# A graph kernel on one Trainium2 core: the second half of the mix layer computed in the edge batches

## The chip, the cores and the metric

The kernel runs on one core of a Trainium2 chip. Its time is in device microseconds (us) of that core, the median of three runs of the same program. Profile and trace come from one further execution, recorded by the hardware profiler. Engines are called by their names: TensorE (PE), VectorE (DVE), ScalarE (ACT), GpSimd (POOL) and SyncE (SP), which here only issues transfers.

## The reference, cut to what matters

`xn` is the layer norm of x, 3125 rows of 256 floats. Three layers are computed from it; the weights are fp32. N = 3125, D = 256, 50,000 edges with three edge types, six node types, eight heads of 32.

```
# edges: every edge takes K and V of its source and Q of its target
K, Q, V = type_proj(xn, node_type, Wk/Wq/Wv)        # a weight matrix for each node type
for t in range(3):
    scores = sum(Wa[t]-turned K[src] * Q[dst], -1) * relation_pri[t] / sqrt(32)
    w      = softmax(scores over all edges of type t)
    msgs  += w * (V[src] @ Wm[t])
gnn = layer_norm(segment_sum(msgs, dst) + xn) * ln_g + ln_b

# mix: linear attention along all rows, then an MLP
q, k, v = split(xn @ Wqkv.T);  q, k = elu(q) + 1, elu(k) + 1
t  = (q @ (k.T v)) / (q . sum(k))
x1 = layer_norm(t + xn) * ln1_g + ln1_b
h  = gelu(x1 @ W1.T + b1)                            # the exact gelu
y  = h @ W2.T + b2
mix = layer_norm(y + x1) * ln2_g + ln2_b

x = x + gnn + mix
x = x + ffn(layer_norm(x))        # up, gelu, down, gated, for the 1561 rows of highest gate score
```

The sums over k and v in the mix attention run over all 3125 rows; the change touches what comes behind x1: h, y and the last layer norm.

## The kernel before

The kernel is written for each engine by hand: every engine has its own program, one instruction behind the other, and semaphores tell an engine when another has done its part. Nothing reorders instructions, so their order in the code of an engine is their order on the chip. The work runs in these stages.

**Front.** x is normalized and node rows are sorted by type.

**Table and mix steps.** A loop of NS + 1 steps runs two things side by side. A tile `t` of 128 sorted nodes gets its K, Q and V rows, which go to tables in DRAM (`kv_scratch`, `q_scratch`); L921 is its K and V product on TensorE, once a step. A tile `m` (NT = 25 of 128 rows) goes through the mix layer, a different part of it in each step: projection and elu, attention, the first layer norm (`shift`, `affine`), `x1T` (the transposed x1, scaled and shifted on ScalarE, L784), `mix_h` (the up product), `gelu` on ScalarE (L794), `mix_y` (the down product), `residual` and `finish` on VectorE (L1300 to L1308: y plus x1 plus bias, statistics, gain), `roots` and `gained` on GpSimd (L667). Exp for the elu and Gelu are in different tables of ScalarE, so that each step has two table loads. The finished row, plus x, goes to `mix_scratch`.

**Edge batches.** 49 batches of eight tiles of 128 edges, as two groups of four tiles. For a group GpSimd issues four gathers of K and V rows from `kv_scratch` (L1425) into a slot of a ring of seven (six in the tensor `big`, one in `wmix`, which held the mix weights). The other engines work on groups of several batches at once, in this order:
- TensorE spreads the target's Q rows (`target_rows`, L1604), sums the messages of a window of targets (`window_sums`, L1621), turns the sums (`turn_sums`, L1630), and makes the types' totals (`totals`, L1639) and maxima (L1648, L1655).
- ScalarE builds the one-hot matrices from distances (L1485 to L1504), copies sums from PSUM (`keep_rows` L1522, `keep_sums` L1528) and takes exponentials (L1513).
- VectorE multiplies K with Q (`products`, L1750), sums per head (L1757), follows the maxima (L1779, L1786, L1793), makes weights (L1800, `mark` L1769), multiplies V by them (`messages`, L1809, two a batch), and searches window bounds (`search`, L1853).
- SP loads the Q rows of windows (L1384) and the keys (L1393).

A slot is free for the next gathers when `window_sums` has read its messages.

**Closing.** The sums of windows are scaled by the softmax factors (VectorE, L2062), turned on TensorE (L2315), copied by ScalarE and stored by SP (L2138) to `agg_scratch`, in 17 units of six groups; `load_part` (L2105) brings the finished mix rows in between, one part of two tiles ahead of each store. GpSimd then gathers the rows (L2203), the second layer norm follows, and the feed-forward layer (L2351 up, L2364 down) ends the kernel.

SP's loop of the closing before the change:

```
for k in range(NU):
    sp.wait_ge(ck_kept, chunks_through(k))      # ScalarE has copied the unit
    ... store of the unit's chunks (L2138) ...
    load_part(k + 2)
    if k == EARLY_AT: ... totals, eight loads of xn rows (L2127) ...
```

Of the kernel before, what the change touches and what calls it, by code (L numbers as in the profile page):

```python
# [10 lines left out]
ALU = mybir.AluOpType  # L11
# [4 lines left out]
P = 128  # L16
# [10 lines left out]
EG = 4  # L27
# [5 lines left out]
RING = 7  # L33
RING_BIG = RING - 1
# [9 lines left out]
SEARCH_AT = 6  # L44
SEARCH_STEPS = 4 + NT + 4
# [30 lines left out]
def build(nc, a, out):  # L76
# [6 lines left out]
    mix_d = scratch("mix_scratch", (NP, D))  # L83
    agg_d = scratch("agg_scratch", (AR, D))
# [5 lines left out]
    with ExitStack() as ctx:  # L90
# [27 lines left out]
        wqT, w1T, w2T = (wmix[:, i * C * D:(i + 1) * C * D].rearrange("p (c o) -> p c o", c=C) for i in range(3))  # L118
        vec_names = ["L0_gnn_ln_g", "L0_gnn_ln_b", "L0_mix_ln2_g", "L0_mix_ln2_b", "L0_mix_b2", "L0_ffn_b2",
# [33 lines left out]
        edge = Arena("edge", 7808)  # L153
# [70 lines left out]
        hT = big.take(2, D)  # L224
        assert big.at <= rel_end
        big.reset(xs_at)
        x2m = big.take(2, D)
        mo = big.take(2, D)
        den = big.take(2, H)
        sts, mvs, rss = big.take(4, 6), big.take(4, 2), big.take(4, 2)  # L230
        nmr = big.take(2)
        x1g = big.take(3, D)
# [16 lines left out]
        kv_slots = [kv[:, s, :, :] for s in range(RING_BIG)] + [wmix[:, :].rearrange("p (k d) -> p k d", k=EG)]  # L249
# [11 lines left out]
        gap = edge.take(4, 64)  # L261
        edge.reset()
# [24 lines left out]
        rows_c = edge.take(NT, D)  # L287
        selT = edge.take(C, ETY, P)
# [10 lines left out]
        junk = edge.take(NHG)  # L299
        edge.reset()  # L300
# [11 lines left out]
        same_t = [vecs[name][0:HW, 0:NHG] for name in ("L0_mix_ln2_g", "L0_mix_ln2_b")]  # L312
        base_f = vecs["L0_mix_b2"][:, 0:NHG + 1]
# [107 lines left out]
        def type_marks(c, dve, in_t, tmp):  # L421
            for t in range(ETY):
# [30 lines left out]
        m_q, m_min, m_exp, m_kf, m_t, m_tx, m_r1, m_rs, m_xh, m_T, m_x1, m_h, m_g, m_y, m_c, m_r2, m_out = (  # L453
            sem(n) for n in ("mix_q", "mix_min", "mix_exp", "mix_kf", "mix_t", "mix_tx", "mix_rstd_1", "mix_shift", "mix_xh",
                             "mix_turned", "mix_x1", "mix_h", "mix_gelu", "mix_y", "mix_stats_2", "mix_rstd_2", "mix_out"))
        m_xin = pair("mix_x_in")
        vmx, pmx, m_xg = sem("mix_step"), sem("mix_pool_step"), sem("mix_x1_gained")
        N_VEC = 5
        mix_vecs = ["L0_mix_b2", "L0_mix_ln2_g", "L0_mix_ln2_b", "L0_gnn_ln_b"]
        mix_vecs += [name for name in vec_names if name in ("L0_mix_ln1_g", "L0_mix_ln1_b")]  # L460
        late_vecs = [name for name in vec_names if name not in mix_vecs]
# [4 lines left out]
        with nc.Block() as block:  # L466
            @block.sync
            def _(sp):
# [88 lines left out]
            def _(pool):  # L557
# [102 lines left out]
                def gained(t):  # L660
                    if t is None:
                        return
                    if t.t == 0:
                        pool.wait_ge(s_pri, 1)
# [1971 lines left out]
```

## Time and profile before

| what | value |
|---|---|
| median of 3 timed runs | 1048.76 us (1048.03 to 1049.56) |
| span of the profiled execution | 1167.3 us |
| TensorE matmul | 967.1 us (83%) |
| VectorE | 803.3 us (69%) |
| GpSimd | 640.5 us (55%) |
| ScalarE | 587.4 us (50%) |
| DMA | 189.89 MB, mean 163 GB/s |

Of the profiled execution there is only the span, 1167.3 us; no time of it by the other clock is shown. It is longer than each of the timed runs, so differences are made against the median and the profile is used for durations and order. The busy shares are averages over stages with different limits.

### The profile page before, as it was taken

To read this page: it belongs to the slowest core of one execution; us is meant where nothing else is said; L and a number is where in the kernel's file an instruction comes from. 1 tells how busy PE (TensorE), PEld (TensorE's weight loads), DVE (VectorE), ACT (ScalarE), POOL (GpSimd) and SP (SyncE) were. 2 spreads that over 40 slices of the span, in tenths; PEclk is the share of its full clock that TensorE was granted. 3 is DMA by queue.
4 is the path that set the end of the run, shared out by engine and by line. 5 is a ranking of instruction groups with operands and counts; after the bars stand their busy time and mean duration, and the time that the engine had idled before them with its cause. 6 is when DMAs were issued, how large, how long until landed. Compare 5 with 4: busy or idle time off the path is not lost.

```text
span 1167.3 us, 18084 instructions
## 1 busy us (share of the span) xinstructions
PE 967.1 (83%) x5053; PEld 677.5 (58%) x5053; DVE 803.3 (69%) x1708; ACT 587.4 (50%) x1534; POOL 640.5 (55%) x818
## 2 busy tenths in 40 slices
PE   5989999997157788777877878778778898999998
PEld 4767777775034444444444444444444687888886
DVE  7755888885256777777767677776767677887541
ACT  2657999983234554555545455554555322322220
POOL 4516788886725666666656666565664025664000
PEclk9999999999565766666667666666776799999999
DMA  9722544444736776766767767677674274210020
GB/s 294 220 71 104 159 145 145 146 146 174 234 114 182 208 212 210 205 204 203 214 202 214 210 198 211 201 211 208 201 211 146 69 226 152 79 46 19 1 86 25
DMA packets 112091, 189.89 MB, mean 163 GB/s; under 512 B 18187, under 2 KB 80734, under 8 KB 111990
## 3 DMA queue, kind: packets, MB, share of 16 engines
q0 software_dynamic: 38992, 129.87, 36.1%
q1 hardware_dynamic: 69718, 55.57, 15.7%
q10 hardware_dynamic: 3280, 3.28, 0.8%
q8 instruction: 43, 0.70, 0.2%
q14 instruction: 58, 0.48, 0.1%
HBM read 154.21 MB, written 34.44 MB: 162 GB/s over the span
## 4 chain that ended last, share of the span: by engine, by line
PE 55%; ACT 12%; issue 11%; another core or an unknown queue 10%; DVE 9%; DMA 1%; SPq 1%; POOL 0%; DVEq 0%; ACTq 0%; POOLq 0%
PE ps L2364 7%; PE ps L1621 7%; PE ps L2351 7%; PE ps L1604 6%; PE ps L921 4%; ACT edge L1500 4%; PE ps L2315 3%; PE ps L932 2%; PE ps L909 2%; PE ps L960 2%; ACT edge L1488 2%; PE ps L985 2%; ACT edge L1485 1%; PE ps L1639 1%
## 5 line engine op out<-in xcount | busy, mean ns | idle before, releaser
L1425 POOL DMA_INDIRECT big<-kv_scratch,src_i x336 | 317.8, 946 | 203.0 <-issue 89.8
L1604 PE MATMUL ps<-edge 64*128 64x256 f32 x784 | 177.6, 595 | 39.0 <-issue 38.8
L1750 DVE TENSOR_TENSOR big<-big,ps 128x1024 f32<-128x1024 f32 x84 | 101.6, 1210 | 121.3 <-PE ps L1604 61.9
L1621 PE MATMUL ps<-big,edge 128*64 128x256 f32 x672 | 149.4, 590 | 19.3 <-issue 10.3
L1604 PEld LDWEIGHTS ps<-edge 64*128 64x128 f32 x784 | 104.7, 289 | 89.5 <-issue 75.1
L1522 ACT ACTIVATE edge<-ps 128x256 f32<-128x256 f32 x98 | 37.6, 383 | 213.3 <-remote 146.0
L1621 PEld LDWEIGHTS ps<-big,edge 128*64 128x64 f32 x672 | 63.2, 199 | 78.6 <-issue 70.0
L1500 ACT ACTIVATE edge<-edge 128x64 f32<-128x64 f32 x392 | 102.9, 334 | 0.0
L1757 DVE TENSOR_REDUCE ps<-big 128x32 f32<-128x1024 f32 x84 | 102.3, 1218 | 0.1
L1809 DVE TENSOR_TENSOR big<-big,ps 128x1024 f32<-128x1024 f32 x84 | 98.9, 1209 | 0.0
L2351 PE MATMUL ps<-big 128*128 128x256 f32 (+2 forms) x416 | 88.7, 368 | 2.8 <-ACT big L2264 2.8
L2364 PE MATMUL ps<-big 128*128 128x256 f32 (+1 forms) x400 | 90.0, 380 | 0.0
L2277 ACT ACTIVATE big<-ps,fb 128x256 f32<-128x256 f32 (+2 forms) x104 | 39.4, 461 | 99.8 <-PE ps L2351 99.8
L1630 PE MATMUL ps<-ident,edge 128*128 128x128 f32 x196 | 53.6, 365 | 41.2 <-ACT edge L1522 32.7
L2351 PEld LDWEIGHTS ps<-big 128*128 128x128 f32 x416 | 74.3, 190 | 11.8 <-ACT big L2264 2.7
L2364 PEld LDWEIGHTS ps<-big 128*128 128x128 f32 (+1 forms) x400 | 73.6, 188 | 10.6 <-issue 0.3
L1425 POOL DMA_INDIRECT wmix<-kv_scratch,src_i x56 | 53.1, 948 | 30.8 <-issue 15.0
L1488 ACT ACTIVATE edge<-edge,ones 128x256 f32<-128x256 f32 x98 | 49.8, 508 | 29.4 <-remote 20.3
L1630 PEld LDWEIGHTS ps<-ident,edge 128*128 128x128 f32 x196 | 23.4, 168 | 68.7 <-ACT edge L1522 51.3
L921 PE MATMUL ps<-big,edge 128*128 x120 | 56.9, 596 | 0.5 <-ACT edge L727 0.3
L1485 ACT ACTIVATE edge<-edge,iota_n 128x256 f32<-128x256 bf16 x98 | 48.7, 497 | 13.9 <-DMA edge<-key_scratch 13.8
L1504 ACT ACTIVATE edge<-edge,ones 128x256 f32<-128x256 f32 x98 | 49.8, 508 | 8.9 <-issue 0.4
(354 smaller groups left out, 1919.0 us busy)
## 6 DMA issues: line engine op xcount, KB each, us to landing
edge<-q_scratch SPq DMA_DIRECT2D x196, 64.0 KB
edge<-key_scratch SPq DMA_DIRECT2D x98, 64.0 KB
big<-kv_scratch,src_i POOLq DMA_INDIRECT x336
agg_scratch<-big SPq DMA_DIRECT2D x16, 252.0 KB
xn_scratch<-big ACTq DMA_DIRECT2D x5, 640.0 KB, 5.4
mix_scratch<-big SPq DMA_DIRECT2D x25, 128.0 KB
big<-xn_scratch SPq DMA_DIRECT2D x25, 128.0 KB, 2.6
edge<-in_x SPq DMA_DIRECT2D x24, 128.0 KB
```

Source lines behind the costliest of these rows:

```text
L921: ins = pe.matmul(ps[1][:, :], xgT[:, t.k, ch * P:(ch + 1) * P], wall[:, ds(ty, 1), ch, 0:2 * D].rearrange("p a o -> p (a o)"), start=(ch ...
L1425: pool.indirect_dma_start(kv_slots[s][:, k, :], None, kv_d[0:N, :], bass.IndirectOffsetOnAxis(ap=src_i[:, e:e + 1], axis=0)).then_inc(got[ ...
L1488: act.activation(ohT[:, g % 2, :], dist, ACT.Relu, bias=ones[:, 0:1], scale=-1.0).then_inc(oh, 1)
L1500: ins = act.activation(gap[:, 2 * k + hg, :], iota_m, ACT.Abs, bias=neg_key[:, e:e + 1])
L1604: ins = pe.matmul(qr_ps[g % 2][:, (2 * hg + k) * D:(2 * hg + k + 1) * D], ohT[64 * hg:64 * hg + 64, g % 2, k * P:(k + 1) * P], qwin[64 * h ...
L1621: ins = pe.matmul(sums_of(g)[64 * hg:64 * hg + 64, :], oneh[:, s, k, hg * 64:hg * 64 + 64], kv_slots[s][:, 2 * hg + k, D:2 * D], start=(k ...
L1630: ins = pe.transpose(sums_of(g)[:, ch * P:(ch + 1) * P], rows_of_sums(g)[:, ch * P:(ch + 1) * P], ident[:, :])
L1750: dve.tensor_tensor(k_rows, k_rows, qr_ps[g % 2].rearrange("p (k d) -> p k d", d=D), ALU.mult).then_inc(pr, 1)
L1757: dve.tensor_reduce(scr[:, g // 2 % 2, (g % 2) * EG * H:(g % 2 + 1) * EG * H].rearrange("p (k h) -> p k h", h=H), kv_slots[g % RING][:, :, ...
L1809: dve.tensor_tensor(v, v, wgt[:, g // 2 % 2, (g % 2) * EG * H:(g % 2 + 1) * EG * H] .rearrange("p (k h d) -> p k h d", h=H, d=1).to_broadc ...
L2351: ins = pe.matmul(hslot[q % 2][:, j * GT * P:j * GT * P + w], fw1[:, ch, f * P:(f + 1) * P], cols[:, ch, at:at + w], start=(ch == 0), stop ...
L2364: ins = pe.matmul(ps[4 + t % 2][0:m, 0:D], fh[:, p % 2, f, at:at + m], fw2[:, f, :], start=(f == 0), stop=(f == FJ - 1))
```

## The change

The mix layer is cut behind x1. In the table steps SP now stores x1T of each tile to DRAM (`mix_x1_scratch`), and the row that goes to `mix_scratch` is only x plus a bias. What follows x1 runs in the edge batches. Tile m belongs to batch F = MIX_FROM[m] = 8 + 3m//2, so 25 of the batches from the eighth on have one. SP loads x1T; at the end of batch F TensorE makes the up product; in batch F + 1 ScalarE makes the gelu and a one-column Exp behind it, TensorE the down product with x1 added by two matmuls with the identity, and VectorE the bias, statistics and gain; SP stores the row to `mix_x2_scratch`. x1T and the row have two places each in `wmix`, so the ring has six slots, all in `big`. In the closing SP loads the rows back two by two behind each store, and GpSimd scales each by its root and adds it to the row of the part (`prepare_row`). VectorE's last combination (`with_rows`) waits for that.

The diff, cut; the new functions are whole but for the fallback of rare inputs, which gets a clearing of semaphores on each engine.

```diff
-RING = 7
-RING_BIG = RING - 1
+RING = 6
+RING_BIG = RING
+MIX_FROM = [8 + 3 * m // 2 for m in range(NT)]
...
@@ SP, table steps
+                    seen(sp, m_x1, t)
+                    sp.dma_start(x1_d[t.t, :, :], x1T[:, t.t % 3, :]).then_inc(m_x1st[t.k], 16)
@@ GpSimd, ScalarE, TensorE, VectorE, table steps: calls taken out
-                    roots(m.at(-5), m_c, m_r2, 1)
-                    gained(m.at(-2))
-                    gelu(m.at(-3))
-                    mix_h(m.at(-3))
-                    mix_y(m.at(-4))
-                    residual(m.at(-5))
-                    finish(m.at(-5))
+                    with_x(m.at(-2))
@@ SP, edge batches
+                def load_x1(m):
+                    at_least(sp, yp, m - 1)
+                    sp.dma_start(x1e[:, m % 2, :], x1_d[m, :, :]).then_inc(x1in[m % 2], 16)
+
+                def store_x2(m):
+                    sp.wait_ge(yg, m + 1)
+                    sp.dma_start(x2_d[m * P:(m + 1) * P, :], x2e[:, m % 2, :]).then_inc(x2st[m % 2], 16)
...
+                    for m in mix_tiles(b, 2):
+                        load_x1(m)
+                    for m in mix_tiles(b, 4):
+                        store_x2(m)
@@ ScalarE, edge batches
+                def mix_gelu(m):
+                    act.wait_ge(hp, m + 1)
+                    at_least(act, yp, m)
+                    for j in range(C):
+                        ins = act.activation(hTe[:, j * P:(j + 1) * P], h_ps_e[:, j * P:(j + 1) * P], ACT.Gelu,
+                                             bias=b1c[:, j:j + 1])
+                    ins.then_inc(hk, 1)
+                    act.activation(back, ones[:, 0:1], ACT.Exp)
...
                     if b >= 0:
                         distances(2 * b + 2)
+                    for m in mix_tiles(b, 1):
+                        mix_gelu(m)
                     keep_rows(2 * b - 3)
@@ TensorE, edge batches
+                def mix_h(m):
+                    pe.wait_ge(x1in[m % 2], 16 * (m // 2 + 1))
+                    at_least(pe, yr, m)
+                    for o in range(C):
+                        for ch in range(C):
+                            ins = pe.matmul(h_ps_e[:, o * P:(o + 1) * P], w1T[:, ch, o * P:(o + 1) * P],
+                                            x1e[:, m % 2, ch * P:(ch + 1) * P], start=(ch == 0), stop=(ch == C - 1))
+                    ins.then_inc(hp, 1)
+
+                def mix_y(m):
+                    pe.wait_ge(hk, m + 1)
+                    for ch in range(C):
+                        pe.matmul(y_ps_e, hTe[:, ch * P:(ch + 1) * P], w2T[:, ch, :], start=(ch == 0), stop=False)
+                    for ch in range(C):
+                        ins = pe.matmul(y_ps_e[:, ch * P:(ch + 1) * P], x1e[:, m % 2, ch * P:(ch + 1) * P], ident[:, :],
+                                        start=False, stop=(ch == C - 1))
+                    ins.then_inc(yp, 1)
...
                     turn_sums(2 * b - 3)
+                    for m in mix_tiles(b, 1):
+                        mix_y(m)
                     totals(b - 1)
                     target_rows(2 * b + 2)
                     window_sums(2 * b - 2)
+                    for m in mix_tiles(b, 0):
+                        mix_h(m)
@@ VectorE, edge batches (mix_row adds the bias, mix_stats, mix_var and mix_gain as their names say)
                     mark(b)
+                    for m in mix_tiles(b, 1):
+                        mix_row(m)
                     messages(2 * b - 2)
+                    for m in mix_tiles(b, 1):
+                        mix_stats(m)
                     messages(2 * b - 1)
+                    for m in mix_tiles(b, 1):
+                        mix_var(m)
+                        mix_gain(m)
@@ SP, closing
+                def load_x2(t):
+                    if t >= NT:
+                        return
+                    at_least(sp, rp, t - 1)
+                    sp.dma_start(x2e[:, t % 2, :], x2_d[t * P:(t + 1) * P, :]).then_inc(x2in[t % 2], 16)
...
+                    load_x2(2 * k + 2)
+                    load_x2(2 * k + 3)
@@ GpSimd, closing
+                def prepare_row(t):
+                    if t >= NT:
+                        return
+                    pool.wait_ge(x2in[t % 2], 16 * (t // 2 + 1))
+                    x2 = x2e[:, t % 2, :]
+                    pool.tensor_scalar(x2, x2, x2r[:, t:t + 1], None, ALU.mult).then_inc(x2g, 1)
+                    pool.wait_ge(mix_in[t // 2 % 3], 16 * (t // 6 + 1))
+                    pool.wait_ge(x2g, t + 1)
+                    pool.tensor_tensor(rows[:, t, :], rows[:, t, :], x2, ALU.add).then_inc(rp, 1)
...
+                for t in range(2 * (HALF_AT + 1)):
+                    prepare_row(t)
@@ VectorE, closing
                 def with_rows(i):
+                    dve.wait_ge(rp, i + 1)
```

ScalarE in an edge batch, before (L1528 copies the turned sums, L1485 and L1488 make distances, L1522 copies window sums, L1513 is the exponential, L1500 and L1504 are one-hots):

```order
L1528 ACTIVATE big<-ps 128x252
L1485 ACTIVATE edge<-edge,iota_n 128x256
L1488 ACTIVATE edge<-edge,ones 128x256
L1522 ACTIVATE edge<-ps 128x256
L1513 ACTIVATE edge<-edge 128x192
L1500 ACTIVATE edge<-edge 128x64 x4
L1504 ACTIVATE edge<-edge,ones 128x256
```

The same place in the first batch with a gelu, with the change; L1500 is now the copy of sums, L1457 and L1460 the distances, L1494 the copy of window sums, L1485 the exponential:

```order
L1500 ACTIVATE big<-ps 128x252
L1457 ACTIVATE edge<-edge,iota_n 128x256
L1460 ACTIVATE edge<-edge,ones 128x256
L1508 ACT_TABLE_LOAD
L1508 ACTIVATE edge<-ps,b1c 128x128 x2
L1511 ACT_TABLE_LOAD
L1511 ACTIVATE edge<-ones 128x1
L1494 ACTIVATE edge<-ps 128x256
L1485 ACTIVATE edge<-edge 128x192
```

Two loads and three activations stand between the distances and the copy of the window sums.

VectorE in an edge batch, before, from the weights of one batch (L1800) to the products of the next (L1750), with one of the search's early steps:

```order
L1800 TENSOR_REDUCE ps<-edge 128x64
L1769 TENSOR_TENSOR edge<-ps,mask 128x192
L1809 TENSOR_TENSOR big<-big,ps 128x4x256 x2
L1835 COPY edge<-ps 124x4
L1836 TENSOR_SCALAR v_L_mix_ln_g<-v_L_mix_b,edge 124x196
```

The same place with the change (L1810 weights, L1779 mark, L1819 messages, L1905 to L1917 the tile's row):

```order
L1810 TENSOR_REDUCE ps<-edge 128x64
L1779 TENSOR_TENSOR edge<-ps,mask 128x192
L1905 TENSOR_TENSOR wmix<-ps,v_L_mix_b 128x256
L1819 TENSOR_TENSOR big<-big,ps 128x4x256
L1909 BN_STATS edge<-wmix 128x6
L1819 TENSOR_TENSOR big<-big,ps 128x4x256
L1913 BN_AGGR v_L_mix_ln_g<-edge 128x2
L1917 SCALAR_TENSOR_TENSOR wmix<-wmix,v_L_mix_ln_g 128x256
L1858 COPY step_f<-edge 128x1
```

The first of the four new operations stands ahead of the messages and needs the down product.

SP at the start of the closing, before: zero rows, then parts of mix rows (L2105) and stores of units (L2138) in turn.

```order
L2129 DMA agg_scratch<-big 128x256
L2130 DMA agg_scratch<-big 69x256
L2105 DMA edge<-mix_scratch 128x2x256 x2
L2138 DMA agg_scratch<-big 126x2x256
L2105 DMA edge<-mix_scratch 128x2x256
```

With the change (L2140 parts, L2155 loads of the mix rows from the edge batches, L2183 stores):

```order
L2170 DMA agg_scratch<-big 128x256
L2171 DMA agg_scratch<-big 69x256
L2140 DMA edge<-mix_scratch 128x2x256 x2
L2155 DMA wmix<-mix_x_scratch 128x256 x2
L2183 DMA agg_scratch<-big 126x2x256
L2140 DMA edge<-mix_scratch 128x2x256
L2155 DMA wmix<-mix_x_scratch 128x256 x2
```

Two loads now stand between each two stores, and each of them waits for a row prepared on GpSimd.

## Rows read from the trace of the kernel before

**Rows 1.** The page, granted TensorE clock in 40 equal slices.

```profile
PEclk9999999999565766666667666666776799999999
```

**Rows 2.** Stretches: from:to, length, busy (count) of PE, PEld, DVE, ACT, POOL; clock; DMA; GB/s.

```profile
97.87:256.40 158.53, 158.06 (x1046) 125.25 (x1045) 125.91 (x359) 147.42 (x284) 125.82 (x173) 1.00 0.41 143
514.70:526.66 11.96, 10.16 (x43) 5.85 (x43) 8.83 (x13) 6.38 (x19) 7.55 (x8) 0.60 0.69 204
342.00:898.30 556.30, 438.82 (x1982) 245.75 (x1984) 402.51 (x585) 294.70 (x874) 347.05 (x372) 0.66 0.69 205
```

**Rows 3.** The page, costliest groups: busy us, mean ns | idle before, releaser.

```profile
L1425 POOL DMA_INDIRECT big<-kv_scratch,src_i x336 | 317.8, 946 | 203.0 <-issue 89.8
...
L1750 DVE TENSOR_TENSOR big<-big,ps 128x1024 f32<-128x1024 f32 x84 | 101.6, 1210 | 121.3 <-PE ps L1604 61.9
```

**Rows 4.** Timeline of two edge batches: start, duration, instruction, idle before.

```profile
504.76 1.08 PE L1621 MATMUL ps<-wmix,edge 128*64 128x256 f32 x8 [0.18 <-issue]
...
510.07 1.97 PE L1621 MATMUL ps<-big,edge 128*64 128x256 f32 x8
...
514.70 0.38 ACT L1522 ACTIVATE edge<-ps 128x256 f32<-128x256 f32 x1 [4.32 <-remote]
514.70 1.22 DVE L1750 TENSOR_TENSOR big<-big,ps 128x1024 f32<-128x1024 f32 x1 [3.54 <-PE ps L1604]
...
516.18 0.94 POOL L1425 DMA_INDIRECT big<-kv_scratch,src_i  x1 [0.30 <-issue]
...
517.38 0.51 ACT L1488 ACTIVATE edge<-edge,ones 128x256 f32<-128x256 f32 x1
...
519.60 0.35 DVE L1793 TENSOR_TENSOR edge<-edge,ps 128x192 f32<-128x192 f32 x1 [0.69 <-issue]
...
521.54 2.34 DVE L1809 TENSOR_TENSOR big<-big,ps 128x1024 f32<-128x1024 f32 x2
...
523.80 0.41 DVE L1853 SCALAR_TENSOR_TENSOR edge<-v_L_mix_b,edge,step_f 128x196 f32<-128x196 f32 x1
```

**Rows 5.** Timeline of ScalarE in a table step: the gelu.

```profile
174.18 1.28 ACT L794 ACT_TABLE_LOAD   x1
175.48 0.63 ACT L794 ACTIVATE big<-ps,b1c 128x128 f32<-128x128 f32 x2
```

**Rows 6.** Timeline of TensorE: L921 in the third and fourth step, and in two later.

```profile
91.49 1.88 PE L921 MATMUL ps<-big,edge 128*128 x4
...
97.87 1.88 PE L921 MATMUL ps<-big,edge 128*128 x4
...
170.03 1.88 PE L921 MATMUL ps<-big,edge 128*128 x4
...
177.27 1.88 PE L921 MATMUL ps<-big,edge 128*128 x4
```

**Rows 7.** Groups on VectorE: the mix row's operations in the table steps.

```profile
L1308 DVE SCALAR_TENSOR_TENSOR big<-big,v_L_mix_ln_g 128x256 f32<-128x256 f32 x25 | 11.5, 460 | 0.0
...
L1300 DVE TENSOR_TENSOR big<-big,v_L_mix_b 128x256 f32<-128x256 f32 x25 | 10.7, 428 | 0.9
...
L1301 DVE BATCH_NORM_STATS2 big<-big 128x6 f32<-128x256 f32 x25 | 10.7, 428 | 0.9
...
L1302 DVE BATCH_NORM_AGGREGATE big<-big 128x2 f32<-128x6 f32 x25 | 4.6, 183 | 0.9
```

**Rows 8.** Timeline of VectorE in the closing: scaling of the units' sums.

```profile
934.42 2.30 DVE L2062 TENSOR_TENSOR big<-big 128x756 f32<-128x756 f32 x2 [0.34 <-PE ps L2315]
...
937.06 2.30 DVE L2062 TENSOR_TENSOR big<-big 128x756 f32<-128x756 f32 x2 [0.34 <-PE ps L2315]
```

**Rows 9.** Groups on GpSimd in the table steps.

```profile
L667 POOL TENSOR_TENSOR big<-big,v_L_mix_ln_g 128x256 f32<-128x256 f32 x25 | 18.0, 719 | 0.1
...
L595 POOL TENSOR_SCALAR edge<-big 128x128 bf16<-128x128 f32 x25 | 16.1, 659 | 6.6 <-DVEq L1092 6.6
```

**Rows 10.** DMA issues of 918 to 975 us: KB each, us to landing.

```profile
big<-xn_scratch SPq DMA_DIRECT2D x8, 128.0 KB, 3.1
```

More of the change, by code:

```diff
@@ L261, in build @@
         gap = edge.take(4, 64)
+        base_f = edge.take(NHG + 1)
+        hTe = edge.take(D)
+        x2s, back = edge.take(6), edge.take(1)
+        assert edge.at <= NT * D + 32
         edge.reset()
@@ L287, in build @@
         rows_c = edge.take(NT, D)
+        edge.take(32)
         selT = edge.take(C, ETY, P)
@@ L299, in build @@
         junk = edge.take(NHG)
+        same_last = edge.take(NHG)
         edge.reset()
@@ L786, in affine @@
                     ins.then_inc(m_x1, 1)
-                def gelu(t):
-                    if t is None:
-                        return
-                    seen(act, m_h, t)
-                    seen(act, m_y, t.at(-2))
-                    for j in range(C):
-                        ins = act.activation(hT[:, t.k, j * P:(j + 1) * P], ps[7][:, j * P:(j + 1) * P], ACT.Gelu,
-                                             bias=b1c[:, j:j + 1])
-                    ins.then_inc(m_g, 1)
                 for s in range(NS + 1):
@@ L1343, in build @@
             s_baseT = sem("bases_turned")
+            x1in, x2st = pair("x1_in"), pair("x2_stored")
+            hp, hk, yp, yr, ya, yv, yg = (sem(n) for n in (
+                "mix_h_ps", "mix_h_gelu", "mix_y_ps", "mix_y_row", "mix_y_stats", "mix_y_var", "mix_y_gained"))
             vd, pd = sem("edge_step"), sem("edge_pool_step")
+            assert [s.num for s in table_sems] == list(range(table_sems[0].num, table_sems[-1].num + 1))
+            for s in table_sems:
+                nc.release_semaphore(s)
+            stage_no[0] += 1
             fb_a, fb_b, fb_c, fb_d, fb_e, fb_f1, fb_g = (sem(n) for n in (
@@ L1369, in build, with mix_tiles @@
             fac_ps = [ps[7][:, 0:ETY * NB], ps[0][:, 0:ETY * NB]]
+            h_ps_e, y_ps_e = ps[0][:, 0:D], ps[0][:, D:2 * D]
+            def mix_tiles(b, lag):
+                return [m for m in range(NT) if MIX_FROM[m] + lag == b]
             def in_range(g):
@@ L2035, in build @@
                 "scaled_first", "scaled_second", "rows_ps", "rows_kept"))
-            ck_st, mix_in = pair("rows_stored"), sem("mix_in")
+            ck_st, mix_in = pair("rows_stored"), [sem(f"x_rows_in{j}") for j in range(3)]
+            x2in, x2g, rp = pair("x2_in"), sem("x2_scaled"), sem("rows_prepared")
+            s_x2r = sem("x2_rstds")
             s_fw, s_head, s_tails = sem("ffn_weights_in"), pair("heads_in"), pair("tails_in")
@@ L2132, in _ @@
                 load_part(1)
+                for i in range(2):
+                    sp.wait_ge(x2st[i], 16 * ((NT + 1 - i) // 2))
+                load_x2(0)
+                load_x2(1)
                 for k in range(NU):
@@ L2215, in _ @@
                 load_tails(0)
+                for t in range(2 * (HALF_AT + 1), 2 * EARLY_AT):
+                    prepare_row(t)
                 pool.wait_ge(sc_first, EARLY_AT)
@@ L2220, in _ @@
                     gather(t)
+                for t in range(2 * EARLY_AT, NT):
+                    prepare_row(t)
                 root(0, v3, mv3, rs3, r3)
```

127 lines of the change are left out of this document (53 added, 74 removed).

## The prediction

> **What bounds the kernel now.** I read the page first, then the stretches of its stages, the groups, and the timeline inside one step of each stage. The page's span is 1167.3 us, and its clock row shows TensorE at full speed for the first ten slices of 29.2 us, at five to seven tenths in the next twenty-one, and full again from about 930 us [rows 1]. The stretches show two regimes [rows 2]: the table and mix steps (97.87 to 256.40) keep TensorE busy 158.06 of 158.53 us and ScalarE 147.42; the edge batches (342 to 898.3) have no engine near full (TensorE 438.8 of 556.3, VectorE 402.5, GpSimd 347.1). The closing behind 919.5 starts with units of row transforms, of which more below.
>
> In the edge batches the reader is to see who waits: VectorE's product of gathered rows (L1750) has 121.3 us idle ahead of it [rows 3], in lumps at the start of each batch. One batch goes from 514.70 to 526.66, 12.0 us. Its start shows VectorE idle 3.54 us and ScalarE 4.32 until the same moment [rows 4]; behind it GpSimd issues eight gathers, 0.946 us each [rows 3] and 0.30 us apart [rows 4], so 8 x 1.25 = 10.0 us. VectorE needs less than that, it is busy 8.83 of the 11.96 us [rows 2].
>
> The profiled execution has only its span to show, and the median of the timed runs is 1048.76 us, 118.5 us less. The idle lumps at L1750 are of just that size [rows 3] (of the batches' groups in slots of `big`; those of the seventh slot come on top); the table steps are filled by TensorE at full clock and have nothing to give. So I take a timed batch to be about 10.0 us, GpSimd's eight gathers, with VectorE 1.2 us below it. Differences worked out below go on the median; on the span they would make 1222 us.
>
> **Table and mix steps.** Removed per tile: eight matmul records of the up product, four of the down product, two gelus, two table loads, the gain and one pair of root operations on GpSimd, five VectorE operations. ScalarE loses 2 x 1.28 us of table loads and 0.63 us of gelu [rows 5]. What a step without the up and down product takes stands in the trace: the third step, whose mix work has not come that far, goes from one L921 to the next in 97.87 - 91.49 = 6.38 us; a full step takes 177.27 - 170.03 = 7.24 us [rows 6]. TensorE is still the bound, so the gain is 0.86 us, not the 3.2 us that ScalarE loses. 22 steps give 19 us, the last ones about 1 more: **-20 us**. Bounds: -12 (if the x1 stores disturb) to -35 (if TensorE's own records alone set the step).
>
> **Edge batches.** 25 of the 49 batches get a tile: two in a row, then one without. VectorE gets four operations: add 0.43, statistics 0.43, aggregate 0.18, gain 0.46 [rows 7], 1.50 us. A batch with a tile is then 8.83 + 1.50 = 10.3 us of VectorE, three batches are 2 x 10.3 + 8.8 = 29.4 against GpSimd's 30.0: own work would be hidden, just. What is not hidden is the wait of VectorE's new first operation for the down product, because VectorE's messages stand behind it. I follow that chain from the end of messages(2b-4), the first of the two in the batch ahead: window sums on TensorE 1.08 at full clock and 0.2 to start; keep_rows, one-hots, keep_sums and distances on ScalarE, from 514.70 to 517.38 + 0.51, 3.2; table load, gelu, table load and a one-column exponential 1.28 + 0.63 + 1.28 + 0.1 = 3.3 [rows 4, 5]; keep_rows 0.38 [rows 4]; on TensorE the turn, the down product, the identity pair and the signal, which I put at 2.1 as an estimate: twice the window sums' 1.08, since the four together stream about twice their columns one after another. Together 10.3 us. In the batch ahead 1.65 us follow messages(2b-4) (one more message, half of 2.34, and the search, 0.41 and its read-out [rows 4]), so the result comes 8.65 us into the batch; VectorE is there after 521.54 - 514.70 less 0.69 idle = 6.15 us [rows 4]. It waits 2.5 us, or 1.3 us in the second batch of a pair, whose forerunner has 1.2 us more behind it. Three batches: 29.4 + 3.8 = 33.2 instead of 30.0, so 3.2 us for two tiles, 12.5 times: 40 us. At the lower clock the same TensorE work takes about twice as long: window sums 1.97 instead of 1.08 [rows 4], in all 2.7 us more per tile, 67 us. I take the full clock nearly alone and put 5 us on: **+45 us**, bounds 0 (the waits fall into idle lumps as those of the profile) and +107.
>
> A table load shows as 1.28 us here, and the next activation starts 0.01 us behind it [rows 5]. The Trainium skill, "ScalarE: Activation LUTs", section "What ACT_TABLE_LOAD costs", counts a drain of about 1.38 us on top, 2.66 us a switch. By that rule each tile would cost 2.8 us more and the edge batches 69 us more; the trace does not agree with it, and the sum goes by the trace.
>
> Six slots instead of seven: a slot's round, from the first gather of a group to the release, takes in this trace seven group times. Behind the issue (5.0 us of four gathers) the rows are wanted two batches ahead of their release; I find no shortage in the timed kernel (20 to 22 us, 5 of issue and about 3 of landing, taken as that of the xn rows, against 30), and put **0** with an upper end of one seventh more time, 100 us if latency alone sets the round.
>
> The x1 loads and x2 stores are 50 x 128 KB on SP's queue, 6.4 MB against some 114 MB that the batches move in 556 us at 205 GB/s [rows 2]: 31 us of transfer at most, hidden while the DMA share is 0.69. SP waits for nothing new that is late.
>
> **Closing.** SP stores a unit of rows each 2.64 us, the spacing of VectorE's scalings of two units (937.06 - 934.42) [rows 8]. In the changed kernel SP must, after each such store, issue two x2 loads, the first only when the row two back is prepared. The round of one of the two buffers is issue 0.4, landing 3.1 as for the xn rows [rows 10], scale, add, then the next issue. The add is 0.72, as the gain on GpSimd was; the scale is 256 wide with a column scalar, which no row shows: at least the 0.66 us of 128 columns, at most twice that, 1.32 us; I take 1.1 [rows 9]. That makes 0.4 + 3.1 + 1.1 + 0.72 + 0.1 = 5.4 us for a unit that took 2.64. Queued behind SP's wait is the next store; ScalarE's copy two units on waits for it, and TensorE for the copy. It holds for units 1 to 11: 11 x 2.75 = 30 us. Before, SP is held up at unit 8 by the early totals and eight xn loads; now it also waits there for GpSimd's five gathers and row 16, and I let the overlap and the new wait cancel: **+30 us**, bounds 0 (short landings, front stores not missed) and +50 (scale and add twice as long beside VectorE's scaling).
>
> **Sum:** -20 + 45 + 0 + 30 = +55; 1048.8 + 55 = 1104 us.
>
> **Rivals.**
> Hidden (faster, 11%): the gelu chain finds its place under GpSimd's 10.0 us a batch, as 29.4 against 30.0 says of the own work, and SP keeps ahead in the closing because x2 rows land in about 1.5 us. Then only the -20 is left: 1029 us, and anything up to 1046. It decides from a wait at the new add of under 0.4 us and a round in the closing under 3 us. Against it: ScalarE's chain is longer than the time that it has.
> Only one of the two costs (27%): the edge batches absorb the tiles, the closing doesn't, or the reverse: 1048.8 - 20 + 30 = 1059, to 1074.
> Low clock or ring (17%): TensorE stays at 1.2 GHz for most of the batches, or six slots become the bound: edge batches +105, 1165 us. For it: the page's clock row [rows 1]; against: the timed batch has not the lumps that the profile's batch has.
> Clock rises (10%): the two window sums near 504.8 and 510.1 ran in 1.08 and 1.97 us at full and half clock [rows 4]. More matmuls in a batch could keep the clock full for more of it, 0.9 us less for each of four such groups; with GpSimd's 10.0 us as floor I count half a us for each of 38 batches back: 1085 us. The Trainium skill, "TensorE: Matmul & The Clock Gate", section "What's actually happening", says that activity releases the throttle and would point to this case.
> The forecast as it stands: 35%.
>
> **Numbers.** 1104 us. The lower neighbours (1059 to 1085) and the upper one up to 1155 belong in the range, which holds about 82%: 1045 to 1158. A measurement of this kernel tells about 0.2%, 2 us, from no change. Slower by more: 0.85; within: 0.03; faster: 0.12.
>
> **What would show it.** After: an L921 spacing near 6.4 us in the table steps; in batches with a tile an idle of 1 to 3 us ahead of the new VectorE add, ended by TensorE; in the closing SP's stores some 5 us apart through unit 11 and ScalarE idle ahead of its copies, ended by those stores. The forecast is wrong if these idles are absent, if gathers become late (VectorE waiting for a landing at L1750), or if the profile's idle lumps exist in timed runs too and swallow the tiles.

## The result, and the profile after

The changed kernel takes **1407.42 us** (median of 4 runs, 1402.84 to 1412.01) against 1048.39 us for the kernel before (1047.73 to 1049.56), a ratio of 1.342 with a 95% interval of 1.338 to 1.345. It is 359 us slower; the forecast was +55, and the range ended at 1158.

The page of the changed kernel: its clock row, as [rows 1], and the groups with the most idle time ahead of them, as [rows 3].

```profile
span 1407.0 us, 18291 instructions
...
PEclk9999999878667676766676676666665897899999
...
L1395 POOL DMA_INDIRECT big<-kv_scratch,src_i x392 | 371.9, 949 | 466.3 <-PE ps L1606 364.4
L1656 PE MATMUL ps<-wmix 128*128 128x128 f32 x200 | 51.9, 441 | 191.3 <-DMA wmix<-mix_x_scratch 191.3
...
L1796 DVE TENSOR_REDUCE mall<-ps 24x1 f32<-24x128 f32 x49 | 13.5, 275 | 235.0 <-PE ps L1633 235.0
```

The gathers (L1395) wait 364 us for window sums, VectorE's maximum (L1796) waits 235 us for TensorE, and TensorE's up product (L1656) waits 191.3 us for x1. I read the first two as consequences and the third as their root, since it is the only one that waits for a transfer and not for another engine; the runs below test that. It is seen in the timeline of one batch F (a selection in order of time, SP's queue among the engines; start, duration, instruction, idle before):

```profile
500.81 0.50 ACT L1457 ACTIVATE edge<-edge,iota_n 128x256 f32<-128x256 bf16 x1
501.33 1.30 SPq L1349 DMA_DIRECT2D edge<-key_scratch  x2
501.76 1.81 PE L1589 MATMUL ps<-edge 64*128 64x256 f32 x8
503.41 4.25 SPq L1340 DMA_DIRECT2D edge<-q_scratch  x4
503.51 1.08 PE L1606 MATMUL ps<-big,edge 128*64 128x256 f32 x8
507.71 0.59 SPq L1354 DMA_DIRECT2D wmix<-mix_x_scratch  x1
511.72 2.08 PE L1656 MATMUL ps<-wmix 128*128 128x128 f32 x8 [7.13 <-DMA wmix<-mix_x_scratch]
...
516.67 0.28 DVE L1796 TENSOR_REDUCE mall<-ps 24x1 f32<-24x128 f32 x1 [8.39 <-PE ps L1633]
```

The x1 load of a tile stands in turn F + 2 of SP's loop. That turn starts with the keys, whose slot is free when ScalarE has read the old ones for the second distances of batch F (501.3). Behind them stand four Q window issues (to 507.7), and only then the x1 load. It lands at 511.7; TensorE wanted it at 504.6 and has the next batch's target rows queued behind the up product.

The stages by the marks of the timelines: the table steps end (first product of the edge batches) at 278.8 us instead of 301.9, and L910, the old L921, comes each 6.37 us instead of 7.24 [rows 6]:

```profile
168.00 1.88 PE L910 MATMUL ps<-big,edge 128*128 x4
174.37 1.88 PE L910 MATMUL ps<-big,edge 128*128 x4
```

In the edge batches those ahead of the first tile take some 10 us (9.9 to 10.4 from the fourth to the eighth), later ones with a tile some 26 and 22.5 us in turn, and those without 9 us. Stretches of the changed kernel, edge batches and closing (columns as in [rows 2]):

```profile
278.80:1108.20 829.40, 502.20 (x2455) 332.56 (x2456) 458.65 (x706) 387.97 (x1031) 365.19 (x389) 0.69 0.52 153
1108.20:1214.40 106.20, 66.48 (x469) 59.38 (x469) 59.65 (x80) 20.40 (x61) 71.81 (x69) 0.83 0.47 142
```

One thing is needed to read the runs below. They fell on several chips, and the kernel before took 1171.67 us on one, 1175.46 on another and 1049.23 on a third. The first two are called "long" chips below, and the third, like the one of the main result, a "short" chip. The profile before, 1167.3 us long, is by its batches from a long chip: a batch takes 12.1 us in it, and 10 us in the profiles from the short chip. Times are compared with the kernel before on the same chip, and stages of profiles only within one kind.

### The profile page after: what moved, and what is told of

It reads as the page before. It is cut to its first block, busy times and chain, and to the rows that moved or that the text cites. A ratio compares the mean times of both kernels' runs of the same rounds, so it can differ in the third digit from the quotient of the medians.

```text
span 1407.0 us, 18291 instructions
## 1 busy us (share of the span) xinstructions
PE 979.9 (70%) x5153; PEld 720.0 (51%) x5153; DVE 786.3 (56%) x1657; ACT 605.3 (43%) x1565; POOL 654.6 (47%) x795
## 4 chain that ended last, share of the span: by engine, by line
PE 41%; ACT 12%; DMA 10%; SPq 10%; issue 10%; POOL 9%; DVE 7%; DVEq 0%; ACTq 0%; POOLq 0%
DMA wmix<-mix_x_scratch 9%; PE ps L2420 6%; PE ps L2433 6%; POOL big L1395 5%; PE ps L1589 5%; SPq L1340 4%; PE ps L1656 4%; PE ps L910 3%; SPq L1339 3%; SPq L1349 2%; ACT L1511 2%; ACT L1508 2%; POOL wmix L2230 2%; PE ps L949 2%; PE ps L1606 2%
## 5 line engine op out<-in xcount | busy, mean ns | idle before, releaser
L1395 POOL DMA_INDIRECT big<-kv_scratch,src_i x392 | 371.9, 949 | 466.3 <-PE ps L1606 364.4
L1656 PE MATMUL ps<-wmix 128*128 128x128 f32 x200 | 51.9, 441 | 191.3 <-DMA wmix<-mix_x_scratch 191.3
L1589 PE MATMUL ps<-edge 64*128 64x256 f32 x784 | 170.7, 575 | 16.4 <-DMA edge<-q_scratch 12.7
L1606 PE MATMUL ps<-big,edge 128*64 128x256 f32 x784 | 133.7, 472 | 26.1 <-ACT big L1500 17.0
L1656 PEld LDWEIGHTS ps<-wmix 128*128 128x128 f32 x200 | 44.5, 328 | 205.5 <-DMA wmix<-mix_x_scratch 205.5
L1500 ACT ACTIVATE big<-ps 128x252 f32<-128x252 f32 x98 | 35.9, 368 | 261.3 <-PE ps L1615 261.3
L1796 DVE TENSOR_REDUCE mall<-ps 24x1 f32<-24x128 f32 x49 | 13.5, 275 | 235.0 <-PE ps L1633 235.0
L1760 DVE TENSOR_TENSOR big<-big,ps 128x1024 f32<-128x1024 f32 x98 | 118.6, 1211 | 16.0 <-DMA big<-kv_scratch,src_i 12.1
L1767 DVE TENSOR_REDUCE ps<-big 128x32 f32<-128x1024 f32 x98 | 119.4, 1218 | 0.1
L1819 DVE TENSOR_TENSOR big<-big,ps 128x1024 f32<-128x1024 f32 x98 | 116.5, 1208 | 0.0
L1494 ACT ACTIVATE edge<-ps 128x256 f32<-128x256 f32 x98 | 37.1, 379 | 139.6 <-PE ps L1606 139.6
L2384 PE MATMUL ps<-bd_m,big 128*126 128x128 f32 (+1 forms) x396 | 53.0, 301 | 22.1 <-ACT big L2319 20.6
```

What stands on the lines that cost most here:

```text
L1395: pool.indirect_dma_start(kv_slots[s][:, k, :], None, kv_d[0:N, :], bass.IndirectOffsetOnAxis(ap=src_i[:, e:e + 1], axis=0)).then_inc(got[ ...
L1589: ins = pe.matmul(qr_ps[g % 2][:, (2 * hg + k) * D:(2 * hg + k + 1) * D], ohT[64 * hg:64 * hg + 64, g % 2, k * P:(k + 1) * P], qwin[64 * h ...
L1606: ins = pe.matmul(sums_of(g)[64 * hg:64 * hg + 64, :], oneh[:, s, k, hg * 64:hg * 64 + 64], kv_slots[s][:, 2 * hg + k, D:2 * D], start=(k ...
L1656: ins = pe.matmul(h_ps_e[:, o * P:(o + 1) * P], w1T[:, ch, o * P:(o + 1) * P], x1e[:, m % 2, ch * P:(ch + 1) * P], start=(ch == 0), stop=( ...
L1760: dve.tensor_tensor(k_rows, k_rows, qr_ps[g % 2].rearrange("p (k d) -> p k d", d=D), ALU.mult).then_inc(pr, 1)
L1767: dve.tensor_reduce(scr[:, g // 2 % 2, (g % 2) * EG * H:(g % 2 + 1) * EG * H].rearrange("p (k h) -> p k h", h=H), kv_slots[g % RING][:, :, ...
```

## The experiments

**1. On a long chip (before: 1171.67 us).** The x1 load one turn earlier:

```diff
-                    for m in mix_tiles(b, 2):
+                    for m in mix_tiles(b, 1):
                         load_x1(m)
```

> The changed kernel with the load of x1 issued one turn of SP's loop earlier, and nothing else changed. Theory A, the load comes too late: the profile of the changed kernel shows TensorE idle 191.3 us ahead of the up product, 25 times 7.65 us, until that load has landed. Without it the idle is gone, and with it what the other engines and the ring lose by it: at least 191 us less, 1216 us, and down to about 1100 us if the rest of a long batch (26.0 and 22.5 us against 9.1 us for one without a tile) was a consequence of the same stall. Rival B, the gelu chain with its two table loads and the down product sets the batch: the idle moves to the copy of window sums on ScalarE and to VectorE's new add, and the time stays above 1300 us. Rival C, six slots make GpSimd wait (364 us ahead of its gathers in the changed kernel): the gathers' wait stays and the time stays near 1400 us.

Measured 1243.35 us, ratio 1.060 (1.055 to 1.064). TensorE no longer waits for x1: its list of waits has none for that load. The changed kernel itself, on the other long chip:

> The changed kernel as it is, beside the variants and beside the kernel before on one chip: in the last runs the kernel before took 1171.67 us where it had taken 1048 us. Theory A (the late x1 load costs the most): the same 7.65 us a tile, so 191 us and more above x1_early's 1243 us: 1430 to 1470 us. If the load costs nothing where the batches are 12.1 us long instead of 10, it is near 1250 us.

Measured 1464.88 us, ratio 1.246 (1.242 to 1.250), beside a kernel before of 1175.46. So the place of one load is worth 222 us of the 289 there, or 218 when each kernel is set against the kernel before on its own chip. Rivals B and C fall as main causes: x1_early is far below the 1300 and 1400 us that they asked for.

The same with a plain bias add for the gelu and no table loads (`ACT.Gelu` to `ACT.Identity`, the Exp behind it out):

> As x1_early, and in the edge batches the gelu is replaced by the plain bias add, and the one-column exponential behind it is left out, so that no table is loaded there; the mix rows are then not the reference's. It prices the table loads once x1 is in time: 2 x 1.28 us and 0.2 us for each of 25 tiles, 69 us if all of it lies on the path. Theory A expects x1_early less 20 to 70 us. Rival B expects most of what the change costs to go here and not in x1_early.

Measured 1208.38 us, 35 less than x1_early, half of the 69 us that the instructions last. The number of slots, in the kernel before (its list of slots is one shorter too):

```diff
-RING = 7
-RING_BIG = RING - 1
+RING = 6
+RING_BIG = RING
```

> The kernel before with six slots instead of seven and nothing else. Theory A: no slot is short, 1048 us plus or minus 5. Rival C: the slot's round sets the batch, a seventh more of some 480 us of batches, about 1115 us.

Measured 1173.97 us, ratio 1.000 (0.997 to 1.004): the seventh slot is worth nothing on a long chip, and rival C falls there.

No tiles at all (`mix_tiles` returns an empty list, no x2 in the closing):

> The changed kernel without any of the work of a mix tile in the edge batches and without the loads and additions of its rows in the closing: what follows x1 in the mix layer is left out altogether. What is left are the shorter table steps, the x1 stores and six slots. Expected from the table steps, whose end moved from 301.9 to 278.8 us in the profiles: 23 us less than before, 1026 us. If six slots cost something, it is above that by as much as before_ring6 shows. Rival C: over 1080 us.

Measured 1145.36 us, ratio 0.980 (0.973 to 0.987), so 26 us less than before where 23 were expected. The 1026 us of the expectation are a time for a short chip.

**2. On another long chip (before: 1175.46 us).** The tile's chain in other places of the batch:

```diff
@@ TensorE                                   @@ ScalarE: behind distances(2 * b + 3), ahead of keep_rows(2 * b - 2)
                     turn_sums(2 * b - 3)
                     for m in mix_tiles(b, 1):
-                        mix_y(m)
+                        mix_h(m)
...
                     window_sums(2 * b - 2)
-                    for m in mix_tiles(b, 0):
-                        mix_h(m)
+                    for m in mix_tiles(b, 1):
+                        mix_y(m)
@@ VectorE
                     maximum(b - 1)
+                    for m in mix_tiles(b, 2):
+                        mix_row(m)
```

Not shown: `mix_gelu` moves as said, `mix_row` leaves its old place, and VectorE's other three operations and the store of the row come one batch later.

> The changed kernel with the tile's chain in other places of the edge batches, all of it still computed: the up product half a batch later, where the down product stood (so x1 has a batch more to land, with the load's place unchanged); the gelu behind the second distances, where ScalarE waits for window sums; the down product at the batch's end behind the second window sums; VectorE's bias add in the batch after, ahead of its second product, statistics and gain behind the messages there. Theory A with its second part, that the rest of the tile's cost is the chain from the up product to the messages of the same batch: no wait of TensorE for x1, none of VectorE at the add, batches with a tile within 1 us of those without; 1171 - 26 + 39 (closing as in x1_early) + 0 to 25: 1184 to 1210 us. Rival D, the tile's own instructions are what costs, wherever they stand: as x1_early, 1240 us or more.

Measured 1230.94 us, ratio 1.049 (1.046 to 1.053): between the 1184 to 1210 us of theory A and the 1240 us of rival D, so neither holds as it was put. TensorE's wait for x1 is down to 25.2 us in all. The edge batches take 638.7 us in its profile, against 660.7 in x1_early and 599.9 in no_tiles, both from the other long chip.

The loads of x2 rows spread out in the closing, on top of x1_early:

> x1_early, and in the closing SP loads a row of x2 behind every second store only, rows 2 to 8 by the 13th, and the others one behind each load of an xn row; GpSimd prepares them in the loop of the feed-forward layer. Theory: SP's wait for prepared rows is what takes the closing from 71 us (last product to first up product, without x2 rows) to 110 us; it falls back to 71 to 80 us and the time to 1243 - 39 = 1204 us, at most 1215. Rival: GpSimd's scale beside VectorE's (2.8 us instead of 0.92) or the bandwidth costs it; then the time stays above 1230 us.

Measured 1234.33 us, 9 less than x1_early and not 39; against the kernel before on each one's own chip it is 13 less (58.9 and 71.7 above it). Its stretches, last product to first up product of the feed-forward layer, and that layer:

```profile
945.20:1020.40 75.20, 64.84 (x479) 56.62 (x476) 58.60 (x77) 21.54 (x62) 41.78 (x35) 0.86 0.56 173
1020.40:1235.30 214.90, 192.53 (x900) 164.78 (x900) 121.01 (x391) 48.99 (x131) 90.28 (x152) 0.96 0.16 50
```

and those of x1_early:

```profile
943.80:1054.20 110.40, 73.83 (x480) 64.89 (x476) 59.06 (x81) 20.88 (x62) 72.54 (x66) 0.76 0.45 137
1054.20:1245.90 191.70, 184.45 (x900) 160.93 (x900) 114.16 (x386) 48.80 (x131) 64.29 (x120) 0.99 0.15 45
```

The theory on SP's wait holds: the units are back at 75 us, 35 less. But the feed-forward stage is 23 us longer. GpSimd now prepares two rows between its roots and its gathers there, some 3.9 us of work, and a round of two gathers takes 11.1 us (1066.19 to 1077.25) instead of 7.6 in x1_early (1095.59 to 1103.22). The two differences, 12 us together, fit the 13.

> chain_moved and closing_spread together. If both theories hold, what is left is the table steps' gain, 26 us by the run without tiles, less what the tiles' own work costs: 1146 to 1170 us, faster than the kernel before by 0 to 2%. If the two costs lean on each other, it is above 1180 us.

Measured 1219.16 us, ratio 1.038 (1.036 to 1.041): the kernel before is not beaten. Above 1180 us the two costs were to lean on each other, but they don't: against each kernel's own before, chain_moved saves 16 us on x1_early, closing_spread 13, and both together 28. Each saving alone is smaller than was expected.

**3. On a short chip, as in the main result (before: 1049.23 us).** The load of x1 moved within its turn:

```diff
                     keys(b + 1)
-                    q_window(2 * b)
-                    q_window(2 * b + 1)
                     for m in mix_tiles(b, 2):
                         load_x1(m)
+                    q_window(2 * b)
+                    q_window(2 * b + 1)
```

> The changed kernel with the load of x1 moved ahead of the two Q windows in the same turn of SP's loop, behind the keys. In the changed kernel that turn begins when ScalarE takes the second distances of batch F (501.3 us in its trace), and then come two key issues (1.3 us), four Q window issues with their register reads (to 507.7), the x1 load (0.6) and its landing (511.7), where TensorE has waited since 504.6. Theory: the order in SP's queue makes the wait, so it falls from 7.1 to about 2 us here (5 us of issues are passed): about 5.1 x 25 = 128 us less than the changed kernel's 1465 us on such a chip, 1300 to 1345 us. Rival: the landing is what is long, whatever stands ahead; then it stays above 1400.

Measured 1241.58 us. On this kind of chip the change takes 1407, so that is 166 us less, where 128 had been expected (the 1300 to 1345 us are times for a long chip). Its list of waits has the up product's wait down to 1.8 us a tile (43.9 over 25), and its timeline shows the load 5 us nearer to the keys:

```profile
498.39 1.30 SPq L1349 DMA_DIRECT2D edge<-key_scratch  x2
499.73 0.59 SPq L1354 DMA_DIRECT2D wmix<-mix_x_scratch  x1
501.10 4.25 SPq L1340 DMA_DIRECT2D edge<-q_scratch  x4
...
503.75 1.51 PE L1656 MATMUL ps<-wmix 128*128 128x128 f32 x8 [2.84 <-DMA wmix<-mix_x_scratch]
```

The rival, a long landing whatever stands ahead, falls: the landing is 4 us in both.

The tiles' instructions and their transfers apart, with the instructions in the places of chain_moved:

> The tiles' chain as in chain_moved, but without their transfers: x1 is not loaded (the up product reads what lies there), the row isn't stored, and the closing has no x2 rows at all. Beside no_tiles (1145 us, edge batches 599.9 us in the profile) and chain_moved (edge batches 638.7 us) it tells whether the 39 us left in the batches are instructions or transfers. Rival D, instructions: edge batches 630 us or more, 1175 us. Theory E, transfers (6.4 MB at about 200 GB/s are 32 us, in a stage that the gathers' landing sets): edge batches 600 to 610 us, 1145 to 1155 us.

> The other half: the 25 loads and 25 stores of 128 KB in the edge batches, and none of the tiles' computing (the stored rows are other data), closing without x2 rows. Theory E: edge batches 630 to 640 us, 1175 us. Rival D: 600 to 605 us, 1146 us.

Measured 1047.56 us without the transfers (ratio 0.998, 0.996 to 1.000) and 1027.01 us with the transfers alone (0.978, 0.975 to 0.981). The latter is 22 us less than before: the gain of the table steps, and neither the transfers nor the missing seventh slot take anything back. On a short chip the transfers are free and the instructions cost 20.5 us even in the better places. Rival D holds there, theory E falls. Only 8 of the 20.5 us can be placed: the edge batches are 498.3 and 490.4 us in the two profiles, but the profiled run of tiles_no_dma took 1037.87 us, 10 less than its median. (The 39 us of chain_moved on a long chip were not split so, and no run on a short chip has both halves in the better places.)

The closing with a shorter round, on top of x1_early (the add's wait for the scale goes too):

```diff
-                    pool.tensor_scalar(x2, x2, x2r[:, t:t + 1], None, ALU.mult).then_inc(x2g, 1)
```

> x1_early with GpSimd's scale of each x2 row left out in the closing (the add stays, so the mix rows are not the reference's). In the trace the scale takes 0.92 us alone and 2.8 us beside VectorE's scaling of sums. If the round of the two buffers (issue, landing, scale, add) sets the closing, a shorter round shows at SP's stores: 110 us of closing become 85 to 95 us, 1220 to 1228 us. If SP's wait for rows has another reason (the gathers ahead of row 16), it stays at 105 us or more.

Measured 1174.17 us, ratio 1.119 (1.115 to 1.123). Its closing is 90.5 us; that of the changed kernel is 106.2 and that of tiles_dma_only, without x2 rows, 67.3 (the expected times were those of a long chip). So the scale is 16 of the 39 us that the x2 rows cost. Edge batches and closing of closing_no_scale:

```profile
280.10:889.60 609.50, 462.37 (x2453) 306.19 (x2453) 457.34 (x706) 387.21 (x1030) 363.67 (x388) 0.76 0.70 208
889.60:980.10 90.50, 67.08 (x472) 59.04 (x472) 63.58 (x80) 20.95 (x62) 41.10 (x44) 0.81 0.56 167
```

and of tiles_dma_only:

```profile
279.40:769.80 490.40, 369.97 (x2044) 213.15 (x2044) 422.81 (x606) 306.92 (x905) 365.45 (x389) 0.80 0.84 258
769.80:837.10 67.30, 59.80 (x479) 53.59 (x479) 54.98 (x76) 21.57 (x62) 13.16 (x16) 0.95 0.56 175
```

## Why the prediction was wrong, by its own steps

The 359 us by stages, from profiles of short chips; the terms make 355 (the end of the old table steps, 301.9, is from a long one; these steps run alike on both, 302.1 in before_ring6 on a chip that ran the batches at 12.1 us):

| term | predicted | measured | from |
|---|---|---|---|
| table steps | -20 | -23 | 278.8 - 301.9; timed -22 and -26 |
| tile chain in its places | +45 | +119 | 609.5 - 490.4 |
| x1 load late | 0 | +220 | 829.4 - 609.5 |
| six slots | 0 | 0 | before_ring6 (a long chip); tiles_dma_only has six and keeps the gain |
| closing | +30 | +39 | 106.2 - 67.3 |

**The step that failed is "SP waits for nothing new that is late".** The prediction priced the x1 loads by their bytes and never placed them in time. It asked whether SP would be held up, not when SP comes to the load and who waits for it: turn F + 2 of SP belongs to batch F of TensorE, so the load has no lead, with four issues ahead. The forecast had a wait ahead of VectorE's add and none ahead of the up product. 191.3 us are the wait itself. The other 29 go with a busier and slower TensorE, which is busy 502 us instead of 462 for the same matmuls, at a mean granted clock of 0.69 instead of 0.76; no run takes the clock's part out by itself. None of the signs that the prediction named looks at this wait: the spacing of 6.4 us, the idle ahead of the add, the slower stores and ScalarE's idle all came, and the largest cost stood beside them.

**The chain's mechanism was right and its size too small.** VectorE in one batch with a tile, closing_no_scale, whose edge batches have the code of x1_early, on a short chip:

```profile
569.19 1.22 DVE L1760 TENSOR_TENSOR big<-big,ps 128x1024 f32<-128x1024 f32 x1
...
572.81 0.28 DVE L1796 TENSOR_REDUCE mall<-ps 24x1 f32<-24x128 f32 x1 [0.72 <-PE ps L1633]
...
574.67 0.35 DVE L1803 TENSOR_TENSOR edge<-edge,ps 128x192 f32<-128x192 f32 x1 [0.46 <-PE ps L1640]
...
578.08 0.38 DVE L1810 TENSOR_REDUCE ps<-edge 128x64 f32<-128x192 f32 x1 [1.92 <-ACT edge L1485]
...
581.14 0.42 DVE L1905 TENSOR_TENSOR wmix<-ps,v_L_mix_b 128x256 f32<-128x256 f32 x1 [2.42 <-PE ps L1665]
...
585.14 1.22 DVE L1760 TENSOR_TENSOR big<-big,ps 128x1024 f32<-128x1024 f32 x1
```

The batch is 585.14 - 569.19 = 15.95 us: about 8.9 us of old work, 1.50 of new, and 5.5 of waits. Missing were the 1.92 at the weights, since ScalarE's exponentials stand behind the gelu as the copy of window sums does, and the 0.72 and 0.46 at the maxima: in this batch the up product stands ahead of what TensorE does for them. (Over the whole run the wait at L1796 is 21.0 us, against 9.6 in tiles_dma_only; tiles_no_dma, with the up product elsewhere, has 20.6, so its place is not shown to be the cause.)

The wait at the add, 2.42, is near the 2.5 of the prediction by luck. Both sides of that difference were some 3.4 us off: VectorE is there 9.5 us into the batch and not 6.15, mostly because of the waits ahead of it, and the result comes after 11.95 us and not 8.65. The chain that leads to the result was put at 10.3 us and takes 13.1, from the window sums at 568.07 to the add. They ran in 1.97 us and not 1.08, ScalarE took 4.0 us and not 3.2 up to the table load, and the turn, the down product and the identity pair, estimated at 2.1, took 3.2:

```profile
568.07 1.97 PE L1606 MATMUL ps<-big,edge 128*64 128x256 f32 x8
...
577.86 0.69 PE L1615 MATMUL ps<-ident,edge 128*128 128x128 f32 x2 [3.22 <-ACT edge L1494]
578.34 1.92 PE L1663 MATMUL ps<-wmix,edge 128*128 128x256 f32 x4
580.04 1.06 PE L1665 MATMUL ps<-ident,wmix 128*128 128x128 f32 x4
```

The wait also comes in the second batch of a pair (2.4 us on average over the 25 tiles), where 1.3 was put. Three batches take 16.0 + 16.2 + 8.8 = 41.0 us, not 33.2. VectorE's work with its waits is the bound, and GpSimd's 10.0 us hide nothing.

**The rival that the clock rises** is not what happened on a short chip: the mean granted clock of the edge batches is 0.80 with the transfers alone, 0.76 with the chain in its places and x1 in time, and 0.69 in the changed kernel. With the same matmuls in the places of chain_moved and no transfers (tiles_no_dma) it is 0.91. On long chips it is 0.66 in no_tiles and 0.75 in x1_early. So more matmuls went with a higher clock in some of these kernels and not in others, and no run separates the clock from the stalls.

**ScalarE's four operations** were priced well. In the same batch their rows are these:

```profile
573.57 0.51 ACT L1460 ACTIVATE edge<-edge,ones 128x256 f32<-128x256 f32 x1
574.09 1.28 ACT L1508 ACT_TABLE_LOAD   x1
575.39 0.63 ACT L1508 ACTIVATE edge<-ps,b1c 128x128 f32<-128x128 f32 x2
576.03 1.28 ACT L1511 ACT_TABLE_LOAD   x1
577.33 0.20 ACT L1511 ACTIVATE edge<-ones 128x1 f32<-128x1 f32 x1
577.43 0.37 ACT L1494 ACTIVATE edge<-ps 128x256 f32<-128x256 f32 x1
```

From first load to the next operation it is 3.34 us, the 3.3 of the sum. The drain of about 1.38 us that the Trainium skill counts on top of a load ("ScalarE: Activation LUTs", section "What ACT_TABLE_LOAD costs") is not in these rows: the first load starts 0.01 us behind the operation ahead of it, and the gelu 0.02 us behind the load.

**Table steps** and **six slots** came as predicted. **Closing**: the mechanism was right, and 39 came for 30. SP's queue in the changed kernel with GpSimd's work, then ScalarE's copy that waits for the store behind it:

```profile
1132.09 4.34 SPq L2155 DMA_DIRECT2D wmix<-mix_x_scratch  x2
1136.48 0.42 SPq L2183 DMA_DIRECT2D agg_scratch<-big  x1
...
1140.05 3.98 SPq L2155 DMA_DIRECT2D wmix<-mix_x_scratch  x2
1144.08 0.42 SPq L2183 DMA_DIRECT2D agg_scratch<-big  x1
```

```profile
1136.07 2.82 POOL L2230 TENSOR_SCALAR wmix<-wmix,v_L_mix_ln_b 128x256 f32<-128x256 f32 x1
1139.04 0.98 POOL L2233 TENSOR_TENSOR edge<-edge,wmix 128x256 f32<-128x256 f32 x1
...
1149.46 0.92 POOL L2230 TENSOR_SCALAR wmix<-wmix,v_L_mix_ln_b 128x256 f32<-128x256 f32 x1 [0.39 <-DMA wmix<-mix_x_scratch]
```

```profile
1147.10 0.66 ACT L2319 ACTIVATE big<-ps 126x256 f32<-126x256 f32 x2 [6.68 <-DMA agg_scratch<-big]
```

These two stores come 7.6 us apart, the widest of the first eight gaps; from the first store (1129.46) to the ninth (1174.74) they are 5.7 us apart on average, near the 5.4 predicted, and 2.64 before [rows 8]. The scale, put at 1.1 us, is 0.92 alone and 2.8 while VectorE scales sums. The term that was mis-sized is the one put at nothing: the early totals and the new wait were said to cancel at unit 8. Instead GpSimd waits for the totals and makes five gathers before it prepares the next row, the next store comes 16.6 us behind the ninth, and ScalarE waits 15.95 us there. Without x2 rows (tiles_dma_only) that gap is 5.3 us, so it costs 11 us.

**The 118.5 us** between profile and timed runs were taken as idle lumps of the profile. Their size was right, and 10.0 us a batch is what short chips show, but the reason was the chip: the timed runs of the kernel before have medians of 1171.67 and 1175.46 us on long chips. (In [rows 1] twenty-two slices are below nine tenths, not twenty-one; nothing rests on it.)

## What to carry to other kernels

A new transfer needs a place in time before a price in bytes: find the instruction whose end lets the queue's turn begin, add the issues ahead and the landing, and compare that with the moment at which the consumer wants it. When work is put into the middle of an engine's order, follow every later instruction of that engine to its consumer and not only the one in the new chain; here three old waits grew beside the one that was expected. A forecast of a difference can also come out while both of its sides are wrong, so compare the sides as well. Where the whole gain is 22 us and the moved instructions alone take 20 of it back in better places, the change has next to nothing to win.

## What the runs showed of the hardware

- The same program takes 1047 to 1052 us on the short chip, and in the main result, and 1164 to 1176 on two others. Nearly all of it is in the edge batches: they take 490.4 us in tiles_dma_only on a short chip and 599.9 us in no_tiles on a long one, 109 of the 116 us between the two profiles. With the same gathers (and 6.4 MB more in tiles_dma_only) they moved 258 and 200 GB/s, at DMA shares of 0.84 and 0.68. Why is open.
- GpSimd's 128x256 scale takes 0.92 us, and 2.8 us when VectorE runs multiplies of two SBUF tensors (L2097) at that time, which are 1.3 us each (six in 7.76 us from 1131.69) and 1.15 us without the scale beside them [rows 8]. The Trainium skill, "SBUF — State Buffer", section "SBUF: two separate sides", says that such a VectorE operation and a GpSimd operation that reads SBUF lock each other out for a whole instruction. The rows agree that each hinders the other; the 1.9 us that the scale loses are more than one multiply, which is not explained here.
- 50 transfers of 128 KB, put into batches that move 241 GB/s without them (tiles_no_dma), cost nothing that can be measured on a short chip: tiles_dma_only is 22 us faster than before, and the table steps alone are 23 us shorter.
